# Three stages of a kernel joined into one block of programs, with a new order on VectorE in the linear attention

## The reference, cut to what matters

```python
x = x + conv_attn(group_norm(x), w_qkv, pos_emb, w_out, b_out)     # 7x7 windows, 4 heads, shift 3, mask
t = tokens(x)
q, k, v = split(layer_norm(t) @ W.T + b)
q = elu(q) + 1.0;  k = elu(k) + 1.0
num = einsum('bti,btij->btj', q, cumsum(k_i v_j, axis=1))
den = einsum('bti,bti->bt', q, cumsum(k, axis=1)) + 1e-06
t = t + num / den
Wx = batch_norm(layer_norm(t) @ Wf.T)
y_t = sigmoid(Wx_t + y_(t-1) @ V.T)                                # one step after the other
t = t + y
```

## Time and profile before

| what | us |
|---|---|
| median of 3 runs (lowest, highest) | 1940.64 (1936.75, 1941.37) |
| the profiled execution | 1940.7 |
| its span, first to last instruction | 1939.0 |
| TensorE busy (its weight loads) | 1869.7 (1577.9) |
| VectorE / ScalarE / POOL busy | 1494.0 / 1192.6 / 1030.0 |
| mean granted clock of TensorE | 0.991 of 2.4 GHz |

### The profile page before, as it was taken

The page is one execution under the profiler, slowest core; times in us unless marked ns, Lnnn a source line. Parts: engine busy times, 40 slices in busy tenths (PEclk is TensorE's granted clock), DMA queues, the critical chain, the costliest instruction groups (busy, mean ns, idle before and its releaser), DMA issues.

```text
span 1939.0 us, 56487 instructions
## 1 busy us (share of the span) xinstructions
PE 1869.7 (96%) x19332; PEld 1577.9 (81%) x19332; DVE 1494.0 (77%) x4515; ACT 1192.6 (62%) x3084; POOL 1030.0 (53%) x1173
## 2 busy tenths in 40 slices
PE   3999999999999999699999999999999998999997
PEld 2888888888888888589999999999999997555554
DVE  7888888888888887477878787878787886355554
ACT  2777777777777777366666666666666664322222
POOL 3888888888888888433333333333333434432330
PEclk9999999999999999799999999999999999999999
DMA  4344443334344332212222222222223223265553
GB/s 138 103 111 109 110 110 107 107 107 110 112 109 109 107 82 78 62 50 67 67 67 63 67 67 67 62 68 67 66 66 113 66 62 103 107 228 187 193 185 121
DMA packets 219629, 192.77 MB, mean 99 GB/s; under 512 B 18264, under 2 KB 189520, under 8 KB 219344
## 3 DMA queue, kind: packets, MB, share of 16 engines
q1 hardware_dynamic: 219344, 189.12, 32.7%
HBM read 111.78 MB, written 77.27 MB: 97 GB/s over the span
## 4 chain that ended last, share of the span: by engine, by line
issue 27%; POOL 15%; PE 15%; DVE 0%; DMA 0%; POOLq 0%; ACT 0%; SPq 0%; DVEq 0%; ACTq 0%
POOL la_rstd L910 11%; PE k_psum L1333 5%; PE k_psum L1324 5%; PE k_psum L1314 3%; POOL la_spread L904 2%; PE k_psum L1341 2%; POOL k_ln_rstd L915 2%; POOLq L40 0%; POOL main_ub L1115 0%; DMA la_masks<-in_masks 0%; ACT main_y L1392 0%; DMA rstd_flat<-sc_turned 0%; PE k_psum L735 0%; DMA sc_scan_rstd<-rstd_flat 0%; PE k_psum L715 0%
## 5 line engine op out<-in xcount | busy, mean ns | idle before, releaser
L904 POOL TENSOR_SCALAR la_spread<-la_mv 128x4 f32<-128x4 f32 x203 | 45.9, 226 | 517.4 <-DVE la_mv L1006 517.4
L555 POOL TENSOR_TENSOR wa_prob<-wa_prob,wa_peak 128x784 f32<-128x784 f32 x128 | 194.6, 1520 | 118.7 <-DVE wa_peak L444 118.6
L853 ACT ACTIVATE la_ve<-k_psum 128x256 f32<-128x256 f32 x196 | 75.3, 384 | 234.3 <-PE k_psum L745 234.3
L910 POOL TENSOR_TENSOR la_rstd<-la_spread,k_exponent 128x4 f32<-128x4 f32 x203 | 209.7, 1033 | 17.4 <-POOL la_spread L904 0.7
L735 PE MATMUL k_psum<-la_uT,la_wt 128*128 128x256 f32 x784 | 203.4, 382 | 0.0
L562 POOL TENSOR_TENSOR wa_prob<-wa_prob,wa_inv 128x784 f32<-128x784 f32 x128 | 194.7, 1521 | 10.2 <-DVE wa_inv L408 10.2
L1392 ACT ACTIVATE main_y<-k_psum,sc_cols 128x512 f32<-128x512 f32 x110 | 75.6, 687 | 201.7 <-PE k_psum L1333 201.7
L1115 POOL TENSOR_TENSOR main_ub<-main_tb,sc_scan_rstd 128x3584 f32<-128x3584 f32 (+7 forms) x21 | 98.2, 4679 | 180.5 <-PE k_psum L1314 179.4
L436 DVE TENSOR_TENSOR wa_prob<-k_psum,wa_bias 128x784 f32<-128x784 f32 x128 | 124.9, 976 | 83.7 <-PE k_psum L291 83.7
L845 ACT ACTIVATE la_raised<-k_psum,la_minus_one 128x512 f32<-128x512 f32 x196 | 134.7, 687 | 65.4 <-PE k_psum L735 65.4
L571 POOL TENSOR_TENSOR wa_xb<-wa_xw,wa_bout 112x512 f32<-112x512 f32 x128 | 164.3, 1284 | 0.0
(11 more groups left out here) (137 smaller groups left out, 5310.8 us busy)
## 6 DMA issues: line engine op xcount, KB each, us to landing
wa_xw<-in_x_tok SPq DMA_DIRECT2D x128, 224.0 KB, 2.6
wa_xT<-in_x_cm SPq DMA_DIRECT2D x128, 196.0 KB, 2.5
la_xc<-x SPq DMA_DIRECT2D x196, 128.0 KB, 2.1
t<-la_tn SPq DMA_DIRECT2D x196, 128.0 KB, 2.1
main_tb<-t SPq DMA_DIRECT2D x13, 1792.0 KB, 7.9
out<-main_ob SPq DMA_DIRECT2D x13, 1792.0 KB, 11.8
x<-wa_y SPq DMA_DIRECT2D x128, 112.0 KB
x<-wa_y SPq DMA_DIRECT2D x128, 56.0 KB
```

The costliest lines, as they stand in the source:

```text
L555: nc.gpsimd.tensor_tensor(s, s, peak[:, k % S, :].unsqueeze(2).broadcast_to([128, PAIRS * HEADS, WIN]), ALU.subtract).then_inc(lowered, 1)
L910: nc.gpsimd.tensor_tensor(rstd[:, n % S, :], spread[:, :], exponent[:, 0:4], ALU.pow).then_inc(rooted, 1)
```

## The change

The window attention no longer has a block of its own. `linear_attention` returns one generator for each engine, and `pipeline` resumes it: once after window step 1 and once after step 3 (the preparation: constants, sum of the weights, folding), and once after each window step from 125 on (on SP from 122), a step of the linear attention each time, the first one n = -4. What is left runs on after the window's last step. The first touch of each PSUM bank waits for the window's last reader of it; two banks change places. SP loads an image of x1 only when that image's stores have landed. At the start the loads of the first eight blocks are issued first by SP, four constants (the group matrix, `w_qkv`, `own` and the identity) go through ScalarE's queue and the other four behind those blocks, VectorE keeps the memsets of the score bank, `ones` and one row of `oT`, and POOL clears the paddings of `xn` and `prob` and all of `vb`. The mask and the bias have two rows (last row of windows, and all others) instead of eight, and the bias is filled in step 0. The scan's tiles and weights lie over the window's tiles; the weights of the recurrence are loaded at linear step 20 instead of 0. In the linear attention VectorE combines the features ahead of the denominators.

```diff
+PREPARE = (1, 3)
...
-def pipeline(eng, step, first, last, lo, hi, unroll=2):
+def pipeline(step, first, last, unroll, following, join):
+    for n in range(first, last):
         step(n, n % unroll)
+        if n in PREPARE or n >= join:
+            next(following)
+    for _ in following:
+        pass
...
+        JOIN = NU - 3
...
+                for n in range(NWR):
+                    load_channels(n, n)
+                sp.dma_start(shift_mask[:, :, :].rearrange("p a b -> p (a b)"), shift_mask_d).then_inc(late_consts, 16)
...
+                def await_image(image):
+                    for k in range(S):
+                        sp.wait_ge(stored[k], stores_before(NWR * (image + 1), k))
+                pipeline(step, **run, following=linear["sync"](sp, await_image), join=JOIN - 3)
...
+                released = dict(u=(q_out, NU), qk=(k_out, NU), v=(v_out, NU), at=(biased, NU), kv=(p_out, 2 * NU),
+                                num=(o_out, NU), gram=(summed, NU))
...
             def _(dve):
+                nc.vector.memset(b_s[:, :, :], 0.0).then_inc(dve_blank, 1)
                 nc.vector.memset(ones[:, :], 1.0)
-                nc.vector.memset(oT[:, :, :, :], 0.0)
-                nc.vector.memset(xn[:, :, :, :], 0.0)
-                nc.vector.memset(vb[:, :, :, :, :, :, :], 0.0)
-                nc.vector.memset(b_s[:, :, :], 0.0)
-                nc.vector.memset(prob[:, :, :, :, :, :], 0.0).then_inc(prep, 1)
-                dve.wait_ge(consts, 128)
+                nc.vector.memset(oT[:, :, WS, :], 0.0).then_inc(dve_blank, 1)
...
             def _(act):
-                act.wait_ge(prep, 1)
-                act.wait_ge(consts, 128)
+                nc.scalar.dma_start(group[:, :], group_d).then_inc(first_consts, 16)
...
+                act.wait_ge(first_consts, 64)
...
             def _(pool):
                 nc.gpsimd.memset(exponent[:, :], -0.5).then_inc(exponent_set, 1)
-                pool.wait_ge(consts, 128)
-                pool.wait_ge(prep, 1)
+                nc.gpsimd.memset(xn[:, :, :, WIN:WPAD], 0.0).then_inc(pool_blank, 1)
+                nc.gpsimd.memset(vb[:, :, :, :, :, :, :], 0.0).then_inc(pool_blank, 1)
+                nc.gpsimd.memset(prob[:, :, :, :, :, WIN:WPAD].rearrange("p k h a b c -> p (k h a b) c"), 0.0).then_inc(pool_blank, 1)
...
-        b_u, b_qk, b_v, b_kt, b_at, b_kv, b_num, b_gram = bank
+        b_u, b_qk, b_v, b_at, b_kt, b_kv, b_num, b_gram = bank
...
                 for n in steps:
                     measure(n + 3)
+                    combine(n)
                     denominators(n - 3)
-                    combine(n)
                     invert(n - 3)
                     normalise(n + 2)
                     aggregate(n + 3)
```

More of the change, by code:

```diff
@@ L94, in build @@
             ffn.normalise_weights(block)
[L95 to L100, removed]
+            scan(nc, block, t2, out, FULL_PLAN, ffn, signals, ident, bank)
+            ffn.compare(block, bank, signals["final_out"], flag, agree)
@@ L101, in build @@
+        again = nc.values_load(flag[0:1, 0:1], min_val=0, max_val=1)
+        with nc.If(again > 0):
             with nc.Fori(0, SEGS - 1):
-                hand_over(nc, start, final)
+                hand_over(nc, ffn.start, ffn.final)
                 clear(nc, signals)
                 with nc.Block() as block:
-                    scan(nc, block, t2, out, MAIN_PLAN, ffn, signals, scan_tiles, ident, bank, start, final)
+                    scan(nc, block, t2, out, MAIN_PLAN, ffn, signals, ident, bank)
@@ L106, in build @@
     top.close()
 def window_attention(nc, x_cm, x_tok, x1, w_qkv, w_out, b_out, shift_mask_d, position_d, ident_d, group_d, own_d,
[L110 to L113 removed]
+                     ident, ones, exponent, psum, bank, ctx, block, linear, ffn):
+    local = ExitStack()
+    if True:
         def sb(name, shape):
[L115 removed]
+            return local.enter_context(nc.sbuf_tensor("wa_" + name, shape, F32))
@@ L197, in softmax_view @@
             return tile[:, k].rearrange("p a b c d -> p (a b c) d")[:, :, 0:WIN]
-        run = dict(first=-AHEAD, last=NU + 6, lo=0, hi=0, unroll=XS)
-        with nc.Block() as block:
+        run = dict(first=-AHEAD, last=NU + 6, unroll=XS)
+        JOIN = NU - 3
+        if True:
             @block.sync
@@ L452, in step @@
                     group_variance(n, k)
+                    set_bias(n)
                     add_bias(n, k)
@@ L518, in step @@
                     exps(n - 1, k - 1)
-                pipeline(act, step, **run)
+                pipeline(step, **run, following=linear["scalar"](act), join=JOIN)
             @block.gpsimd
@@ L579, in step, with linear_attention @@
                     keep_tokens(n - 1, k - 1)
-                pipeline(pool, step, **run)
-def linear_attention(nc, ctx, block, x1, t2, attn_wt, attn_b, masks_d, ident, ones, exponent, ln2_rstd, gram, bank,
-                     ffn, signals, scan_tiles, ffn_data):
+                pipeline(step, **run, following=linear["gpsimd"](pool), join=JOIN)
+def linear_attention(nc, ctx, x1, t2, attn_wt, attn_b, masks_d, ident, ones, exponent, ln2_rstd, gram, bank,
+                     ffn, signals, ffn_data):
     if True:
@@ L1241, in _, with scan @@
                 pool.sem_clear(semaphore)
-def scan_buffers(nc, ctx, name):
-    def sb(label, shape):
-        return ctx.enter_context(nc.sbuf_tensor(f"{name}_{label}", shape, F32))
-    return dict(tb=sb("tb", [SEGP, 4, NG, LONGEST, C]), ub=sb("ub", [SEGP, 2, NG, LONGEST, C]), ob=sb("ob", [SEGP, 2, NG, LONGEST, C]),
-                uT=sb("uT", [128, 2, COLS]), y=sb("y", [128, 2, COLS]))
-def scan(nc, block, t2, out, plan, ffn, signals, tiles, ident, bank, start, final):
+def scan(nc, block, t2, out, plan, ffn, signals, ident, bank):
+    tiles, start, final = ffn.tiles, ffn.start, ffn.final
     tb, ub, ob, uT, y = (tiles[label] for label in ("tb", "ub", "ob", "uT", "y"))
```

187 lines of the change are left out of this document (115 added, 72 removed).

## The result

| | before | after | predicted |
|---|---|---|---|
| median (lowest, highest), us | 1939.15 (1936.75, 1941.37) | 1893.05 (1891.56, 1893.94) | 1892 (1880 to 1912) |
| profiled execution / span | 1940.7 / 1939.0 | 1892.84 / 1891.0 | 1892.6 |
| ratio of the times, 95% interval | | 0.9762 (0.9748, 0.9776) | |
| TensorE busy | 1869.7 | 1844.3 | |
| POOL busy | 1030.0 | 1034.3 | |

The kernel is faster by 46.1 us, and the profiled span is shorter by 48.0. In what follows one execution of the last experiment (2254.72 us at a mean granted clock of 0.794, where its others have 0.995 or 0.996) is left out. To see where, the span is cut at four events of TensorE that both traces have: the first matmul of the window's keys, the scores of the last block (127), queries and keys of unit 6, and those of unit 195.

A forecast was written before the change was run, and what follows sets the result against it. TensorE was taken to set the pace, giving away a tenth of a microsecond per unit to VectorE's order, with VectorE bounding the start. 1940.7 - 12.5 + 2.4 - 18 - 20 = 1892.6, stated as 1892, range 1880 to 1912.

The forecast's parts named there:

- units of 3.98, not 4.10: Rival, linear attention: the unit stays at 4.10 us because another wait takes the place; 1910 us, chance 0.11.
- no mutual wait of POOL and VectorE: Rival, both seams: POOL and VectorE wait for each other, transition saves 11, preparation costs 3.5; 1900 us, chance 0.10.
- VectorE's wait for ScalarE: Slower rival, linear attention: the combination waits for ScalarE ahead of the denominators; 1977 us at worst, chance 0.03.
- The start: Before the first window keys: less VectorE clearing and bias work, earlier loads; 12.5 us saved, bounds 11 and 13.5.
- so the transfers now decide: At the start: VectorE keeps about 1.5 us of memsets, so block transfers, landed at 9.5 to 11.7, set the pace.
- The preparation: After window step 1: folding the linear attention's weights there delays VectorE's step 2; 2.4 us lost, bounds 1 and 3.5.
- The seam: Window to linear attention: drain, barrier, constant loads and fold gone, first steps interleaved; 18 us saved, bounds 11 and 24.
- I let half of that reach the chain: In the seam: one VectorE normalisation meets POOL's lowering and weighting (1.52 us each); half of that delays the chain.
- The 15 that I worked out by the rule: In the seam: if each of three normalisations waits out POOL's whole queue, the saving is some 15 us.
- I count these even: Seam, unit 0 to 6: relief from 1.2 GHz balances 4.1 us of window work and the waits for weighting 127.
- The order: Linear attention: combination ahead of denominators ends the score matmuls' wait, unit becomes 4.00; 20 us saved, bounds 4 and 24.
- The rest: After unit 195, with the recurrence: the scan is unchanged, 0 us foreseen.

The follow-up runs named there:

- e1: The changed kernel with VectorE's combination put back behind the denominators, nothing else undone; 1917.6 us, ratio to before 0.9885.
- e3: The changed kernel with the linear attention's steps starting only after the window's last step, no interleaving; 1897.7 us, ratio 0.9788.
- e4: The changed kernel with the joined steps beginning one window step earlier (from 124, on SP from 121); 1890.74 us, ratio 0.9754.
- e5: The changed kernel with the preparation moved from window step 1 to step -2, its three loads to SP's step -5; 1890.13 us, ratio 0.9742.
- e2: The kernel before with the combination ahead of the denominators, nothing else changed; 1913.69 us, ratio 0.9869.
- e6: The changed kernel with POOL's three clearings (5536 elements) given to VectorE; 1894.59 us, ratio 0.9761.
- e8: e7 with blocks 8 and 9 loaded ahead of four late constants, and two useless matmuls before the preparation's; 1889.4 us, ratio 0.9741.
- e9: Also "the last experiment": e8 without its useless matmuls, the preparation's three loads issued by ScalarE's queue; 1888.75 us, ratio 0.9739.
- e7: The changed kernel with both the early preparation of e5 and the earlier join of e4; 1888.65 us, ratio 0.9738.

## Why the prediction was right

**The mechanisms of the order and of the joining hold, and three sizes were off.** The port was charged and held nobody, and two things put at nothing cost time, the bias beside the first normalisation and the clock in the seam. The rivals are gone: units of 3.98, not 4.10; no mutual wait of POOL and VectorE, which would have left the seam at 46 (57.25 - 11); and VectorE's wait for ScalarE is there, but hidden.

**The start**, 12.5 foreseen, 10.80 measured, just outside the bounds of 11 to 13.5; by the traces of e1, e3 and e4, with the same start, it is 11.34, 10.84 and 11.23. The failing step is "I take 12.5 us saved". The normalisation was foreseen at 12 to 14, and came at 14.06 (13.53 to 14.03 in those three), the late end. The price of POOL's memset was bounded by 3.47 and 8; it was 3.52, so this uncertainty fell away. The sum's first step, "so the transfers now decide", holds in part. In the kernel after they do until 7.74, then VectorE's own queue does, with five blocks, the aggregate and two more blocks, until 12.3; in e1, e3 and e4 VectorE waits again for the transfer of block 8, and measures block 9 from 11.25 (e1) and 11.36 (e4), within the 9.5 to 11.7 that the transfers were given. And the saving was read at the normalisation instead of at the keys. The bias was moved to step 0 at no cost, but it stood beside POOL's first normalisation and stretched it from 0.68 to 1.15, so that the keys came 1.30 behind its start, not 0.73.

**The preparation**, 2.4 foreseen, 2.05 measured; e5 shows that it was this. The wait foreseen on TensorE (about 2) was 2.32.

**The seam**, 18 foreseen, 15.18 measured, inside 11 to 24. Two steps were off. "I let half of that reach the chain" charged 1.5 for the port. The trace has the collision: the two normalisations from 783.06 on took 0.84 and 1.55, 2.31 in all instead of 0.58, beside the two POOL operations. But they held only VectorE. POOL had work without a gap from 781.29 on, and came to VectorE's next results, the statistics and the inverse of block 127, only at 786.49 and 787.80, though they were there at 785.54 and 786.67; so nothing of it reached TensorE. The rule of the Trainium skill (SBUF — State Buffer, "Who interferes with whom"), that in a two-port mode VectorE and GpSimd exclude one another, agrees with this row, as far as it goes: 783.06 + 2.31 is 785.37, and POOL's pair ends at 785.29. In which mode VectorE worked, no row shows. The 15 that I worked out by the rule is close to the 15.18 for another reason, which is the second step: "I count these even". From the turn of 126 to queries and keys of unit 0 it took 5.0 instead of 3.2, much of it at 1.2 GHz (2.05 for 1.04 in the projection), after a turn that itself was 0.4 late behind the values of unit 0; and unit 0 to unit 6 took 27.29, not 25.07, although the order had made units 4 and 5 shorter by 0.54. The relief from 1.2 GHz was real (the granted clock is 1.00 from 790 on), but the window's leftovers cost more: TensorE waits 0.92 and 0.98 for the tokens' copy on ScalarE, 0.92 for the state's, 0.17 and 0.55 for that of the attended block, all in the first three units. With 4.4 lost (0.4 + 1.8 + 2.2) and 1.5 not paid at the port, 18 becomes 15.1.

**The order**, 20 foreseen, 22.48 measured. The mechanism is shown by e1 and e2: 299 ns for 275 or 276. The sum held 18.1 + 1.0 and "0.01 or 0.02 a unit in the delayed start", that is 1.9 to 3.8 over 189 units; written as 20 they were rounded down, since the three give 21.0 to 22.9. Over the whole kernel the order is worth more, 24.6 (e1 against after) to 25.5 (e2 against before) by the medians. The next wait foreseen, the second outer product for the state, is small: in the whole stage the weight loads of the outer products wait 0.4 us for the state.

**The rest**, 0 foreseen: 1.59. The change is not shown to have made it: e2, which has the order alone, takes 313.96 there, and the other kernels with the new order 314.33 to 315.95, so traces of nearly the same work lie 2 us apart.

Errors of -1.7, +0.35, -2.8, +2.5 and +1.6 add to nothing. That the time was met to 1 us is thus partly chance; that the range held is not, for each term but the first kept its bounds. The range itself was not what the terms allowed: at their worst bounds, 11, 3.5, 11 and 4, they give 1918, not "about 1906".

Of the signs named, three came: the wait of 2 us behind step 1 (2.32), the mean of 275, the unit of 4.00 (3.98). Four did not: the first keys near 13 (15.36), no stretch at 1.2 GHz (3.4 us), unit 0 some 30 us earlier (26.15), and denominators that still wait for the numerators.

## What to carry to other kernels

An engine at 99% busy can still hide a tenth of a microsecond in each step: compare the mean length of matmuls of the same shape, and where one group is longer, look whether its stationary operand is written just in time, and what stands ahead of the instruction that writes it. If an operand can be made early, put its instruction before the one that waits longest, since the wait then covers it. When stages are joined, work that only prepares belongs where all engines wait anyway, and the join should begin early enough that the in-order engines (ScalarE here) don't put the old stage's wait in front of the new stage's first operand.

## What the runs showed of the hardware

- POOL cleared 4096 float32 elements per partition in 3.52 us and 960 in 0.90; VectorE takes 3.47 and 0.86 for the same (e6). POOL's tensor operations here are much slower (1.52 for 784 elements), so they are no guide to its memsets.
- VectorE and POOL stretched each other, in both directions: two normalisations on VectorE took 0.84 and 1.55 us instead of 0.58 together beside two POOL operations (after, 783.06), and one on POOL took 1.15 instead of 0.68 beside VectorE's bias additions (after, e1, e3, e4 and e6; 0.68 in e8 and e9, where the bias comes later).
- The granted clock fell to 1.2 GHz about a wait of 2.61 to 2.63 us, for 3.4 us in one trace (after) and 6.8 in three others (e1, e5, e6). In e8 it fell behind waits of 1.55 and 0.72, in e7 not, with 1.56 and 0.73 in the same sequence; the two falls of e8 cost 2.7 us together.
- A transfer issued 0.6 us earlier, on ScalarE's queue instead of SP's, landed 2.6 us later (e9 against e7, one trace of each).
